# Decoder steps rewritten on small tiles, with the context products between the two convolutions on TensorE

## The reference, cut to what matters

```
def step(carry, tgt):
    s, c, alpha = carry                       # state, cell: [16,128]; alignment: [16,128]
    f = conv1d(alpha, conv_w)                 # 101 taps
    e = einsum('a,bta->bt', va, tanh(enc_proj + (s @ Wa_s.T)[:, None, :] + f_projected + ba))
    alpha_new = softmax(where(mask, e, -1e30), axis=1)
    g = einsum('bt,btd->bd', alpha_new, hbatch)
    rec = tgt @ L_ys.T + s @ L_ss.T + g @ L_gs_w.T + L_gs_b      # [16, 512]: four gates
    ig, fg, cg, og = split(rec, 4)
    c_next = sig(fg) * c + sig(ig) * tanh(cg)
    s_next = sig(og) * tanh(c_next)
```

## Time and profile before

| | us |
|---|---|
| median of 3 runs | 4213.84 (4213.58 to 4214.56) |
| profiled execution, its own time | 4207.08 |
| span in its trace | 4205.3 |
| the 128 steps, about | 2185 to 3712 of the span |

### The profile page before, as it was taken

One profiled execution on the slowest core, in us unless ns is written; L12 is line 12 of the kernel. 1 busy time (PEld: TensorE's weight loads), 2 busy tenths in 40 slices (PEclk: granted clock), 3 DMA queues, 4 the chain that ended last, 5 costly groups with the idle time before them and its releaser, 6 DMA issues. The chain is left out here.

```text
span 4205.3 us, 66878 instructions
## 1 busy us (share of the span) xinstructions
PE 3526.3 (84%) x21282; PEld 1828.8 (43%) x21354; DVE 2660.2 (63%) x6647; ACT 1564.5 (37%) x3710; POOL 504.9 (12%) x1854
## 2 busy tenths in 40 slices
PE   6546478444599999995989999999999999974998
PEld 4424155222376777772533333333333333322554
DVE  2665767588655555553227777777777777764443
ACT  2221144354322222221115555555555555532222
POOL 0000511233200010000000000000000000023222
PEclk9566689777799999998999999999999999976888
DMA  2000020200100000001013233333233233211000
GB/s 92 3 2 8 2 46 8 83 0 0 42 1 0 0 0 0 0 0 51 15 39 82 78 81 82 78 82 82 78 82 82 78 82 82 78 33 46 25 25 30
DMA packets 272180, 176.49 MB, mean 42 GB/s; under 512 B 17054, under 2 KB 258216, under 8 KB 272056
## 3 DMA queue, kind: packets, MB, share of 16 engines
q1 hardware_dynamic: 269368, 172.54, 14.4%
q0 software_dynamic: 2752, 3.18, 0.5%
HBM read 164.94 MB, written 13.90 MB: 43 GB/s over the span
## 5 line engine op out<-in xcount | busy, mean ns | idle before, releaser
L1783 PE MATMUL ps<-st_hk,de_wct 112*128 112x512 f32 x1024 | 525.9, 595 | 14.3 <-DVE st_lss L1903 13.1
L1849 ACT ACTIVATE st_th<-st_pre,st_sw 128x128 f32<-128x128 f32 x1024 | 327.2, 390 | 552.7 <-DVE st_sw L1908 552.7
L1804 PE MATMUL ps<-de_hg,st_at 128*32 128x512 f32 x4096 | 492.5, 598 | 0.3 <-DVE st_at L1939 0.3
L1922 DVE SCALAR_TENSOR_TENSOR st_th<-ps,st_sw,de_enc 128x128 f32<-128x128 f32 x1024 | 288.5, 345 | 30.1 <-DVE st_sw L1908 0.4
L1798 PE MATMUL ps<-st_lss,st_sT 128*128 128x512 f32 x512 | 288.1, 645 | 0.0
L1952 DVE TENSOR_TENSOR st_rec<-ps,st_rin 128x256 f32<-128x256 f32 x512 | 193.3, 418 | 125.9 <-PE ps L1804 125.9
L1783 PEld LDWEIGHTS ps<-st_hk,de_wct 112*128 112x128 f32 x1024 | 189.1, 205 | 140.5 <-DMA st_hk<-padded_alignments 72.2
L1764 POOL COPY de_ah<-st_at 128x8 f32 (+1 forms) x256 | 51.0, 199 | 1656.6 <-DVE st_at L1939 1656.6
L1247 PE MATMUL ps<-sa_xt,w_wq 128*128 128x128 f32 x2048 | 237.9, 278 | 1.9 <-ACT sa_xt L1363 1.9
L1247 PEld LDWEIGHTS ps<-sa_xt,w_wq 128*128 128x128 f32 x2048 | 234.7, 194 | 11.0 <-issue 9.2
L1318 PE MATMUL ps<-sa_wo,sa_ct 128*128 128x512 f32 x512 | 225.0, 598 | 13.1 <-issue 13.1
(11 more groups left out here) (402 smaller groups left out, 6412.7 us busy)
## 6 DMA issues: line engine op xcount, KB each, us to landing
st_hk<-padded_alignments SPq DMA_DIRECT2D x508, 224.0 KB, 3.2
X<-in_x_dram SPq DMA_DIRECT2D x16, 512.0 KB, 12.0
out_dram<-X SPq DMA_DIRECT2D x16, 512.0 KB, 2.7
padded_alignments<-st_al SPq DMA_DIRECT2D x508, 2.0 KB
w_wq<-in_Wq_perm_dram SPq DMA_DIRECT2D x1, 4096.0 KB, 18.0
sa_wo<-in_Wo_perm_dram SPq DMA_DIRECT2D x1, 4096.0 KB, 14.5
gate_inputs<-dp_ro SPq DMA_DIRECT2D x16, 256.0 KB, 2.0
st_rin<-gate_inputs SPq DMA_DIRECT2D x256, 16.0 KB
```

Of the source, the lines that this page charges most:

```text
L1783: pe.matmul(ps[:, CV[g] + i, :], wct[:, :], hk[g][:, 4 * i:4 * i + 4, :].rearrange("p b n -> p (b n)"), start=True, stop=True).then_inc(co ...
L1804: ins = pe.matmul(R[g][32 * j:32 * j + 32, :], at[g][:, j, i, :], hg[:, BG * g + 4 * i + j, :], start=False, stop=(i == 1), tile_position= ...
L1849: ins = act.activation(th[g][:, b, :], pre[g][:, b, :], ACT.Tanh, bias=sw[g][:, b:b + 1])
L1922: ins = dve.scalar_tensor_tensor(out=th[g][:, b, :], in0=ps[:, CV[g] + 1, (b - 4) * P:(b - 3) * P], scalar=sw[g][:, b:b + 1], in1=enc[:, B ...
```

## The change: what it does

The steps are written anew. The gate sum now lies with a quarter of the 512 gate columns in each quarter of the rows and one sequence every four rows, so that it is 128x128. It is transposed (`turn_gates`), and from there the cell works on tiles of 128x8, and writes the state in the layout in which TensorE reads it. The encoder term isn't added on VectorE after the convolution any more: VectorE copies `enc` into PSUM ahead (`fill`), and the convolution adds onto it. Factors of a half that were applied in the steps are moved into the weights. The alignment goes out in one DMA in place of two.

TensorE's order in a half is new too: `state_term(o)`, `turn_alignment(g)`, `convolve(o, m, 0)`, `gates_of_context(g)`, `convolve(o, m, 1)`, `gates_of_state(o)`, `mask(o)`, `energy(o, m, 0)`, `turn_gates(g)`, `energy(o, m, 1)`.

```diff
-            rin = pair("rin", [P, U5, 512])
+            rin = pair("rin", [P, U5, P])
-            pre = pair("pre", [P, BG // 2, P])
-            rec = pair("rec", [P, 512])
-            gt = pair("gt", [P, 512])
+            rec = pair("rec", [P, P])
+            gt = pair("gt", [P, 4 * BG])
-            c1, c2, cc, tc, s2 = pair("c1", [P, P]), pair("c2", [P, P]), pair("cc", [P, P]), pair("tc", [P, P]), pair("s2", [P, P])
-            sT = pair("sT", [P, P])
+            c1, c2, cc, tc = pair("c1", [P, BG]), pair("c2", [P, BG]), pair("cc", [P, BG]), pair("tc", [P, BG])
+            sT = pair("sT", [P, 32])
...
                     def convolve(g, n, i):
+                        pe.wait_ge(filled[i][g], n + 1)
                         pe.wait_ge(hk_in[i][g], 16 * n)
-                                  start=True, stop=True).then_inc(conv_ps[g], 1)
+                                  start=False, stop=True, skip_group_check=True).then_inc(conv_ps[i][g], 1)
...
                     def gates_of_state(g, n):
-                        pe.matmul(R[g], sT[g][:, :], lss[:, :], start=True, stop=False, skip_group_check=True)
+                        for q in range(4):
+                            pe.matmul(R[g][32 * q:32 * q + 32, :], sT[g][:, :], lss[:, q * P:(q + 1) * P],
+                                      start=True, stop=False, tile_position=(0, 32 * q), skip_group_check=True)
                     def gates_of_context(g, n):
                         pe.wait_ge(at_ready[g], n + 1)
-                        for i in range(2):
-                            for j in range(4):
-                                ins = pe.matmul(R[g][32 * j:32 * j + 32, :], at[g][:, j, i, :], hg[:, BG * g + 4 * i + j, :],
+                        for b in range(BG):
+                            for q in range(4):
+                                ins = pe.matmul(R[g][32 * q:32 * q + 32, :], at[g][:, b, :], hg[:, BG * g + b, q * P:(q + 1) * P],
...
+                    def turn_gates(g, n):
+                        pe.wait_ge(rec_ready[g], n + 1)
+                        pe.transpose(T[g], rec[g][:, :], ident[:, :]).then_inc(t_ps[g], 1)
...
                     def half(g, n, o, m, u, more):
                         if front:
                             state_term(o, m)
+                        turn_alignment(g, n)
+                        if front:
+                            convolve(o, m, 0)
                         gates_of_context(g, n)
                         if front:
-                            energy(o, m)
+                            convolve(o, m, 1)
                             gates_of_state(o, m)
-                        if more:
-                            convolve(g, n + 1, 0)
+                            mask(o, m)
+                            energy(o, m, 0)
+                        turn_gates(g, n)
                         if front:
-                            turn_alignment(o, m)
-                        if more:
-                            pe.wait_ge(s_rows[g], n + 1)
-                            pe.transpose(ST[g], s2[g][:, :], ident[:, :]).then_inc(st_ps[g], 1)
-                            convolve(g, n + 1, 1)
+                            energy(o, m, 1)
...
+                    def fill(g, n, i):
+                        dve.wait_ge(th_done[g], 2 * n) if not (isinstance(n, int) and n == 0) else dve.wait_ge(cleared, 4)
+                        dve.tensor_copy(CV[g][i], enc[:, BG * g + 4 * i:BG * g + 4 * i + 4, :].rearrange("p b n -> p (b n)")).then_inc(filled[i][g], 1)
+                    def add_state(g, n):
+                        dve.wait_ge(conv_ps[1][g], n + 1)
+                        dve.wait_ge(sw_ready[g], n + 1)
+                        dve.tensor_tensor(th[g][:, 4:8, :], rows4(CV[g][1]), sw[g][:, 4:8].unsqueeze(2).broadcast_to([P, 4, P]),
+                                          ALU.add).then_inc(added[g], 1)
...
                         if front:
                             keep_state_term(o, m)
-                            add_all(o, m)
+                        keep_alignment(g, n)
+                        if more:
+                            fill(g, n + 1, 0)
+                        if front:
+                            add_state(o, m)
+                        if more:
+                            fill(g, n + 1, 1)
                         dve.wait_ge(r_sum[g], n + 1)
+                        dve.tensor_tensor(rec[g][:, :], R[g], rin[g][:, u, :], ALU.add).then_inc(rec_ready[g], 1)
                         if front:
                             top(o, m)
+                        dve.wait_ge(gates_done[g], n + 1)
```

More of the change, by code:

```diff
@@ L1701, in cols, with by_batch, states, rows4 @@
-            def cols(v):
-                return v.rearrange("p (j c) -> p c j", c=32)[:, 0:2, :]
+                f = v[:, :, :].rearrange("p b c -> p (b c)")
+                return bass.AP(f.tensor, f.offset, [list(f.ap[0]), [36 * 4, 2], [36, 4]])
+            def by_batch(v):
+                return v.rearrange("p (j i c) -> p i j c", i=2, c=16)[:, :, :, 0]
+            def states(g):
+                return sT[g][:, 0:32:4]
+            def rows4(v):
+                return v.rearrange("p (b n) -> p b n", n=P)
@@ L1778, in state_term @@
                         pe.wait_ge(st_ready[g], n + 1)
[L1779 removed]
+                        pe.matmul(SW[g], was[:, :], states(g), start=True, stop=True).then_inc(sw_ps[g], 1)
                     def convolve(g, n, i):
+                        pe.wait_ge(filled[i][g], n + 1)
                         pe.wait_ge(hk_in[i][g], 16 * n)
[L1783 to L1784 removed]
@@ new lines, in mask, with energy @@
+                    def mask(g, n):
+                        pe.wait_ge(sw_ready[g], n + 1)
+                        pe.matmul(E[g], ident16[:, :], mask16[:, g, :], start=True, stop=False, skip_group_check=True)
+                    def energy(g, n, i):
+                        pe.wait_ge(th_done[g], 2 * n + i + 1)
+                        for j in range(4):
+                            ins = pe.matmul(E[g][32 * j:32 * j + 32, :], vas[:, i, :], th[g][:, 4 * i + j, :],
+                                            start=False, stop=(i == 1), tile_position=(0, 32 * j), skip_group_check=True)
+                        if i == 1:
+                            ins.then_inc(e_ps[g], 1)
@@ L1832, in _ @@
                         for i in range(2):
-                            convolve(g, 0, i)
+                            pe.matmul(CV[g][i], wct[:, :], hk[g][:, 4 * i:4 * i + 4, :].rearrange("p b n -> p (b n)"),
+                                      start=True, stop=True).then_inc(cleared, 1)
+                    for i in range(2):
+                        convolve(0, 0, i)
                     state_term(0, 0)
-                    energy(0, 0)
                     gates_of_state(0, 0)
-                    turn_alignment(0, 0)
+                    mask(0, 0)
+                    for i in range(2):
+                        energy(0, 0, i)
                     steps(pe, half)
@@ L1901, in _ @@
                     done(dve.tensor_copy(ident16[:, :], ident[:, :]))
-                    done(dve.tensor_scalar(lss[:, 0:3 * P], lss[:, 0:3 * P], 0.5, None, ALU.mult))
+                    done(dve.tensor_scalar(lss[:, 0:3 * P], lss[:, 0:3 * P], 0.25, None, ALU.mult))
+                    done(dve.tensor_scalar(lss[:, 3 * P:4 * P], lss[:, 3 * P:4 * P], 0.5, None, ALU.mult))
+                    done(dve.tensor_scalar(was[:, :], was[:, :], 0.5, None, ALU.mult))
                     assert len(setup) == SETUP
@@ L1967, in half @@
                         dve.wait_ge(tc_done[g], n + 1)
-                        dve.scalar_tensor_tensor(out=s2[g][:, :], in0=to, scalar=1.0, in1=tc[g][:, :], op0=ALU.add,
-                                                 op1=ALU.mult).then_inc(s_rows[g], 1)
                         if more:
-                            add_encoder(g, n + 1)
-                        if front:
-                            keep_alignment(o, m)
-                        if more:
-                            dve.wait_ge(st_ps[g], n + 1)
                             dve.wait_ge(hist_s[g], n + 1)
-                            dve.tensor_scalar(sT[g][:, :], ST[g], 0.5, None, ALU.mult).then_inc(st_ready[g], 1)
+                            dve.scalar_tensor_tensor(out=states(g), in0=to, scalar=1.0, in1=tc[g][:, :], op0=ALU.add,
+                                                     op1=ALU.mult).then_inc(st_ready[g], 1)
                     state = {}
                     for g in range(G5):
-                        add_encoder(g, 0)
+                        for i in range(2):
+                            fill(g, 0, i)
                     keep_state_term(0, 0)
-                    add_all(0, 0)
+                    add_state(0, 0)
                     link = Chain(dve, dve_seq)
@@ L1987, in _ @@
                     align(link, 0, 0)
-                    keep_alignment(0, 0)
                     def start(it):
```

123 lines of the change are left out of this document (46 added, 77 removed).

## The result

| | before | after |
|---|---|---|
| median, us | 4213.71 (4208.75 to 4214.56, 4 runs) | 5058.99 (5053.57 to 5066.05, 4 runs) |
| profiled execution / span | 4207.08 / 4205.3 | 5053.57 / 5051.8 |
| clock over the steps | 1.00 | 0.87 |

The changed kernel takes 1.201 times as long (95% interval 1.1989 to 1.2031), 845 us more. The median lies 72 us above the forecast and inside its range.

What follows compares the result with a forecast made beforehand. A chain through TensorE and VectorE was taken to set the half at 8.05 us, with a partly lowered clock 8.98: 4207.1 + 773 = 4980, and 6.8 more for the median gives 4987 us, range 4690 to 5180.

Steps and rivals of the forecast that it cites:

- TensorE alone: TensorE's own instruction list in a half: 5.53 us, 0.42 us shorter than before, the most the change could bring there.
- Chain, steps 1 to 5: From state term through both convolutions, `add_state`, `fill` and gate sum to `turn_gates`, which starts at 5.91 us.
- Step 6: Second tanh and last energies: the transpose ahead holds the energies until 6.07 us, and they end at 6.49.
- Step 7: Maximum at 6.55 us, through reciprocal, alignment (7.57) and state (7.83) to the next state term at 8.05 us.
- The clock: TensorE's pauses bring 1.2 GHz for 30% of the time, so a half goes from 8.05 to 8.98 us.
- the factor 0.69: TensorE's busy share of a half, 5.53 in 8.05 us, used to size the work slowed at the lower clock.
- The once-only parts: Shorter clearing of `rin` and two or three small multiplications more: a few us either way, taken as zero.
- B: Rival: same chain, but the clock stays up; 8.05 us per half, 4750 us; chance 0.19.
- C: Rival: TensorE's 97 instructions a half, instead of 43, come too slowly; about 5080 at 20 ns more each; chance 0.09.
- D: Rival: the lower clock for over half of the time, 9.94 us a half, 5230 us; chance 0.05.
- E: Rival: TensorE's own list sets the half at 5.53 us, 107 us less, 4107 us; chance 0.04.
- B with its slower fill: What the prediction said its range, 4690 to 5180 us, takes in: the chain with the clock up and a slower `fill`.

Runs made afterwards that it cites:

- the best order: Changed kernel with the first convolution half a step ahead, the second before the context products, gate sum before second fill, gates of the state behind turned gates: 4138.15 us.

## Why the prediction was right, and where it was off

**TensorE alone.** 5.53 us a half was close: the best order runs at 5.65. Context products take 1.884 us from their first start to the convolution's at the full clock, where 1.92 was taken. One piece was short: `turn_gates` takes 0.26 to its successor, and not 0.16.

**Chain, steps 1 to 5.** `add_state` was forecast at 4.35 and starts at 4.39; `fill` at 4.96 and 5.00; gate sum at 5.57 and 5.59; `turn_gates` at 5.91 and 5.93. The 0.69 for a copy of 128x512 into PSUM was right (686 ns), not the lower 0.47.

**Step 6.** The last energies start at 6.19, not 6.07, for the short piece above. **Step 7** was too long by 0.06: from the alignment to the state it is 0.20. Together 8.12 for 8.05 us. With the pauses filled the chain costs 552 us; 536 was the forecast.

**The clock** is the term that was mis-sized. 0.93 us a half was forecast (8.98 - 8.05), 237 us; it is 294 us, 1.15 a half. The prediction chose 30% of the time at the lower level, between 0 and the 40% that it drew from long stretches. Over the steps the mean of 0.87 is 26%, so the time was about right, which is partly luck, since no row decided between 0 and 40. What failed is the factor 0.69 for TensorE's work in it: the low stretch does not lie evenly over work and pauses but begins with the work that follows the long pause, where all of it is on the chain. 0.26 x 9.29 / 2 = 1.21 us, near the 1.15 measured, where the forecast's form would give 0.26 x 0.69 x 9.29 / 2 = 0.83. The two errors, a share too high and a factor too low, partly cancelled, so the forecast of the clock's cost came nearer than its terms. The forecast's mechanism, a slower chain plus a lower clock that its pauses bring, is what was measured, and so are the signs that it named: `add_state` waits, the gate sum doesn't, and the clock is 0.87.

**The once-only parts** were taken as zero. Nothing measured shows them apart; chain and clock together leave about nothing for them (4213.7 + 552 + 294 = 5060).

**Rivals.** B was the chain alone, 4750: the kernel with full pauses shows just this state, at 4765. C fell, since the 64 instructions took 29 ns each. D, over half of the time at the low clock, did not come about. E, TensorE's list setting the half, needed the gate sum at once behind the context; VectorE's list held it back by 2.3 us, where 2.2 was forecast, and only other orders came near E's time. The range's lower end, called "B with its slower fill" in the prediction, is B with the faster fill, 0.47 us (4214 + 479 = 4693); the fill took 686 ns. The Trainium skill, TensorE: Matmul & The Clock Gate, section Back-to-back issue gap, gives some 81 ns per matmul for a stream of weight loads and matmuls of 128 columns, by which the context would be an estimated 5.2 us. The trace disagrees for these packs: 64 f32 instructions in 1.884 us are 29 ns each, with four side by side on quarters of the array.

## What to carry to other kernels

Where several engines walk through fixed lists, ask of each instruction not only what it costs but who is held up behind it: two convolutions of 0.9 us each, moved from "half a step ahead" to "just in time", cost 812 of the 845 us over 255 halves, while the list they stand in got shorter (5.95 us before, 5.65 in the fastest order here). Here the chain that opened pauses on TensorE cost twice, once for itself and once for the clock in the work behind the pause, and the two can be told apart by filling the pauses with matmuls that nobody reads, in a loop body that doesn't outgrow the instruction supply. When work is done ahead of time, check whether its input is ready by then, and move only as much ahead as that allows.

## What the runs showed of the hardware that was not expected

- With a TensorE loop body of 1680, 1792 or 2032 matmuls and weight loads, every pass starts with a wait of the engine for its instructions, 2.2 to 3.1 us on the mean, and 3.1 to 3.7 MB go over the instruction queue in 1600 us. With 1552, and with 840, there is no such wait and no such traffic over the steps. It is a matter of the number of instructions and not of more work: the two kernels with 1792 wait 2.5 us (256 columns in each filler) and 3.1 us (8 columns).
- In the changed kernel the lower clock came as single stretches of 3.4 us at 1.2 GHz, in 183 of 255 halves: two or three slow halves, then one at the full clock. Why one half has it and the next, with the same pauses, has not, stays open. With the same 1.5 us pause at the half's end, the clock went with the pause ahead of `turn_gates`: none, 0.98; 0.70 us, 0.87; 1.57 us, 0.78.
